# Two attentions in float32: key blocks that a DMA lays out, products on row halves and column strips of the array

## The reference

```
x = x + tanh(g_xattn[0]) * _L0_xattn_ref(_layernorm(x), ctx_512, ctx_512)   # 8 key heads of 8 numbers, 4 query heads each
x = x + tanh(g_ffn[0])   * _L0_ffn_ref(_layernorm(x), ...)                  # 64 experts, the best 8, and a shared one
x = x + tanh(g_xattn[1]) * _L1_xattn_ref(_layernorm(x), ctx_512, ctx_512, Wc, bc)  # 4 key heads of 16 numbers, 4 query heads each
x = x + tanh(g_ffn[1])   * _L1_ffn_ref(_layernorm(x), w_fc, w_proj)
# an attention: scores = einsum("bkgsd,bktd->bkgst", qh, kh) * scale; attn = softmax(scores); out = einsum("bkgst,bktd->bkgsd", attn, vh)
```

## Time and profile before

| | us |
|---|---|
| three runs | 1705.94, 1711.78, 1712.32 |
| their median | 1711.78 |
| span of the profiled execution | 1714.7 |

### The profile page before, as it was taken

One profiled execution on the slowest core, in us unless ns is written; L12 is line 12 of the kernel. 1 busy time (PEld: TensorE's weight loads), 2 busy tenths in 40 slices (PEclk: granted clock), 3 DMA queues, 4 the chain that ended last, 5 costly groups with the idle time before them and its releaser, 6 DMA issues.

```text
span 1714.7 us, 32329 instructions
## 1 busy us (share of the span) xinstructions
PE 1178.8 (69%) x9122; PEld 778.6 (45%) x9132; DVE 1084.7 (63%) x2699; ACT 783.1 (46%) x1599; POOL 883.5 (52%) x846
## 2 busy tenths in 40 slices
PE   4999998133333299999678777871676777846775
PEld 2566665112221266666555555650454444532243
DVE  5899996666666466666444454442765555747898
ACT  3566665122222166666445454441343333433574
POOL 2343343266666633333377777715888888516100
PEclk9999999555555599999777887785788888878878
DMA  9555554032323599999899999984344434100011
GB/s 209 161 151 154 148 154 135 15 115 104 111 106 110 154 281 308 310 301 304 206 242 237 252 246 248 247 199 101 53 54 55 55 55 55 28 1 1 13 37 49
DMA packets 283470, 247.09 MB, mean 144 GB/s; under 512 B 117584, under 2 KB 270032, under 8 KB 282960
## 3 DMA queue, kind: packets, MB, share of 16 engines
q1 hardware_dynamic: 234192, 169.99, 38.9%
q0 software_dynamic: 49152, 75.53, 20.8%
HBM read 111.93 MB, written 117.77 MB: 134 GB/s over the span
## 4 chain that ended last, share of the span: by engine, by line
DMA 24%; DVE 20%; PE 18%; POOL 16%; issue 13%; SPq 4%; ACT 3%; DVEq 1%; POOLq 0%; ACTq 0%
DMA xs<-V 13%; POOL x L632 11%; DMA arena<-xs 8%; PE bank L1493 4%; DVE arena L1318 3%; DMA xs<-arena,V 2%; PE bank L1369 2%; POOL rs L575 2%; PE bank L1381 2%; DVE arena L971 2%; PE bank L1355 2%; PE bank L1569 2%; PE bank L1370 2%; SPq L518 2%; DVE arena L1316 2%
## 5 line engine op out<-in xcount | busy, mean ns | idle before, releaser
L632 POOL DMA_INDIRECT x<-ys,idx x256 | 404.1, 1578 | 129.2 <-issue 57.6
L650 POOL DMA_INDIRECT xs<-V x192 | 187.1, 974 | 207.7 <-DMA xs<-V 188.5
L1493 PE MATMUL bank<-arena,region 128*128 128x128 f16 x2496 | 253.2, 245 | 1.6 <-ACT arena L834 0.9
L834 ACT COPY arena<-bank 128x640 f16<-128x640 f16 x192 | 132.3, 689 | 190.2 <-PE bank L1569 188.2
L1569 PE MATMUL bank<-arena 128*128 128x128 f16 x1440 | 145.2, 240 | 105.3 <-DMA arena<-xs 101.5
L1381 PE MATMUL bank<-arena 128*72 128x256 f32 (+1 forms) x768 | 212.0, 417 | 0.1
L1493 PEld LDWEIGHTS bank<-arena,region 128*128 (+1 forms) x2496 | 187.0, 111 | 19.2 <-issue 6.2
L1569 PEld LDWEIGHTS bank<-arena 128*128 128x128 f16 x1440 | 97.0, 107 | 113.3 <-DMA arena<-xs 85.4
L573 POOL TENSOR_TENSOR ve<-mv,epsilon 128x1 f32<-128x1 f32 x96 | 39.5, 412 | 202.0 <-DVE mv L912 180.0
L1381 PEld LDWEIGHTS bank<-arena 128*72 128x72 f32 (+1 forms) x768 | 117.2, 158 | 46.4 <-issue 13.5
L982 DVE TENSOR_REDUCE arena<-bank 128x8 f32<-128x512 f32 x192 | 124.1, 675 | 15.5 <-PE bank L1355 14.3
(11 more groups left out here) (204 smaller groups left out, 2557.6 us busy)
## 6 DMA issues: line engine op xcount, KB each, us to landing
ys<-arena SPq DMA_DIRECT2D x96, 512.0 KB
arena<-xs SPq DMA_DIRECT2D x288, 160.0 KB
xs<-idx SPq DMA_DIRECT2D x52, 256.0 KB, 2.4
arena<-in_wpairs SPq DMA_DIRECT2D x32, 256.0 KB, 2.6
arena<-in_wpairs SPq DMA_DIRECT2D x128, 64.0 KB, 2.5
x<-ys,idx POOLq DMA_INDIRECT x256, 6.3
out<-arena SPq DMA_DIRECT2D x16, 256.0 KB, 2.2
xs<-idx SPq DMA_DIRECT2D x52, 64.0 KB, 2.1
```

Source lines behind the costliest of these rows:

```text
L632: pool.indirect_dma_start(tile_x(t), None, ys[t // HT], bass.IndirectOffsetOnAxis(ap=idx[:, t, k:k + 1], axis=0), compute_op=ALU.add).then ...
L650: pool.indirect_dma_start(xs[t // HT], bass.IndirectOffsetOnAxis(ap=at_row[:, t, n % 8:n % 8 + 1], axis=0), ROW[t % NROW], None).then_inc( ...
L834: act.copy(XTP[g % 2][q], tpm[n % 2]).then_inc(R_["xt"], 1)
L1493: mm = pe.matmul(o, lhs(a, w, k), rhs(a, w, k), start=(n == 0), stop=(n == 3 * KT - 1))
```

## The change

- Queries, maxima and keys stay float32. The high and low parts go, and with them `KH`, `KL`, the mask table, L971, L1028, the casts of the keys and one of the two normalisations (`query`).
- Key blocks: four buffers `KD`, zeroed once. SP writes the diagonal blocks of a tile by DMA out of HBM, one DMA per key head (8 in layer 0, 4 in layer 1), each of 8 or 16 partitions by two runs of 64 numbers. The rows that take off the maximum come by 8 DMAs of their own per layer (`own_rows`). For layer 1, POOL zeroes the buffers after layer 0, and SP fills them in the middle of the experts (`g == NG`).
- The array is used in parts: half of the key heads on rows 0 to 63, the other half on rows 64 to 127, in two banks. Scores have 64 rows by 128 columns, maxima 32 rows by 64 columns, values 128 rows by strips of 32 (layer 0) or 64 columns (layer 1).
- Order: PE begins a step with the turning of tile `t + 2` and takes half of its maxima in step `t`. ACT casts the experts' weights at the end of a step, no longer between the exponentials. POOL fills `VD` in layer 0.

The core of the diff:

```diff
-    KH = sb("KH", [P, B, S], F16)
-    KL = sb("KL", [P, B, S], F16)
+    KD = [sb(f"KD{n}", [P, 2, 4 * S]) for n in range(NKD)]
...
-    XG = [carve([G, C + W0]) for _ in range(2)]
-    KM = carve([2 * 8 * S], F16)
-    Q1 = [carve([G, P], F16) for _ in range(2)]
-    Q2 = [carve([G, P], F16) for _ in range(2)]
-    KD1 = [carve([2, 8 * S], F16) for _ in range(2)]
-    KD2 = [carve([2, 8 * S], F16) for _ in range(2)]
-    VD = [carve([2, 4 * W0]) for _ in range(2)]
+    XG = [carve([G, P]) for _ in range(NKD)]
+    Q = [carve([G, P]) for _ in range(NKD)]
+    VD = [carve([2, P]) for _ in range(2)]
...
+            def own_rows(layer):
+                nk = LAYERS[layer][0]
+                a = CW + RCW + TCW + layer * 4 * S
+                for q in range(NKD):
+                    for r in range(2):
+                        at = slice(r * OWN + C // 2, r * OWN + C // 2 + nk // 2)
+                        sp.dma_start(KD[q][at, :, 0:nk // 2 * S],
+                                     consts[at, a:a + nk // 2 * S].unsqueeze(1).to_broadcast([nk // 2, 2, nk // 2 * S])).then_inc(d_own, 16)
+
+            def keys(t, layer):
+                nk, d = LAYERS[layer]
+                if t >= NKD:
+                    sp.wait_ge(A[layer]["sc_ready"], (t - NKD + 1) * nk // 2)
+                for k in range(nk):
+                    r, i = k // (nk // 2), k % (nk // 2)
+                    sp.dma_start(KD[t % NKD][r * OWN + i * d:r * OWN + (i + 1) * d, :, i * S:(i + 1) * S],
+                                 ctxT[k * d:(k + 1) * d, 2 * t * S:2 * (t + 1) * S].rearrange("c (b s) -> c b s", b=2)).then_inc(d_kd[t % NKD], 16)
...
+            sp.wait_ge(kd_zero, NKD)
+            own_rows(0)
+            for t in range(2):
+                keys(t, 0)
...
                 pair(n, stage[n], d_stage[n])
-            keys(1)
+            for t in range(2, NKD):
+                keys(t, 0)
             sp.dma_start(x[:, 4:12, :], xv[:, 4:12, :]).then_inc(d_x[1], 16)
             values(1)
             sp.dma_start(x[:, 12:NT, :], xv[:, 12:NT, :]).then_inc(d_x[2], 16)
...
+                if n + 2 < NT:
+                    keys(n + 2, 0)
                 sp.wait_ge(wlo_done, 2 * (n - 1))
                 if n > 2:
                     sp.wait_ge(d_w, 80 * (n - 2))
...
+                if g == NG:
+                    sp.wait_ge(kd_zero, 2 * NKD)
+                    own_rows(1)
+                    for t in range(NKD):
+                        keys(t, 1)
                 if NG <= g < NGG and (g - NG) % 6 == 0:
...
+            for t in range(NKD, NT):
+                keys(t, 1)
...
+                        if past(t, 0):
+                            pool.wait_ge(a["pv_ready"], t + 1)
+                            stand_alone(pool, side_v)
+                        pool.tensor_tensor(VD[j].rearrange("p b (n h w) -> p (b n) h w", h=2, w=P // nk)[:, :, :, 0:d],
+                                           V[:, bass.ds((t + 2) * 2, 2), :].rearrange("p b (n h d) -> p (b n) h d", h=2, d=d),
+                                           ones[:, 0:2].unsqueeze(1).unsqueeze(3).to_broadcast([P, 2 * npair, 2, d]), ALU.mult).then_inc(a["vd_ready"], 1)
...
+            for q in range(NKD):
+                pool.memset(KD[q][:, :, :].rearrange("p b t -> p (b t)"), 0.0).then_inc(kd_zero, 1)
...
+                def step(t, q):
+                    j = q % 2
+                    if inside(t + 2):
+                        act.wait_ge(a["t1_ready"], t + 3)
+                        act.copy(Q[(q + 2) % NKD], bank[0].rearrange("p (g s) -> p g s", g=G)).then_inc(a["q_ready"], 1)
                     if inside(t):
-                        for u in range(nsc):
+                        for u in range(2 * nsc):
                             exps(t, j, u)
...
-                    if inside(t):
-                        for u in range(nsc, 2 * nsc):
-                            exps(t, j, u)
...
+                    if layer == 0 and inside(t):
+
+                        if known(t) and t < 2:
+                            act.wait_ge(d_stage[t], 80)
+                        else:
+                            act.wait_ge(d_w, 80 * (t - 1))
+                        act.copy(gu_view(t, 0), stage[j][0].rearrange("p m e i -> p e m i")).then_inc(whi_done, 1)
+                        act.copy(RW[:, bass.ds(2 * t, 2), KT * P:SW], stage[j][1]).then_inc(whi_done, 1)
...
+                def first_step(t, q):
+                    j = q % 2
                     if inside(t + 1):
-                        for u in range(nmx // 2):
-                            maxima(t + 1, 1 - j, u)
+                        maxima(t + 1, (q + 1) % NKD, 0)
+                        maxima(t + 1, (q + 1) % NKD, 1)
+                    if inside(t + 3):
+                        if known(t) and t == -3:
+                            dve.wait_ge(d_x[0], 16)
+                        if known(t) and t in (1, 3):
+                            dve.wait_ge(d_x[(t + 1) // 2], 16)
+                        dve.bn_stats(st[:, 1 - j, :], tile_x(t + 3)).then_inc(LNA["stats"], 1)
...
+                        inverse(t - 1)
+                    if inside(t + 3):
+                        dve.wait_ge(LNA["stats"], t + 4)
+                        stand_alone(dve, side_v)
+                        dve.bn_aggr(mv[:, 1 - j, :], st[:, 1 - j, :]).then_inc(LNA["mv"], 1)
+                    if inside(t - 1):
+                        weighted(t - 1, 1 - j)
                     if inside(t + 1):
-                        for u in range(nmx // 2, nmx):
-                            maxima(t + 1, 1 - j, u)
+                        maxima(t + 1, (q + 1) % NKD, 2)
+                        maxima(t + 1, (q + 1) % NKD, 3)
...
+                def maxima(t, q, gp):
+
+                    n = t * nmx + 2 * gp
+                    if past(t, 1) or gp >= 1:
+                        pe.wait_ge(a["mx_done"], n)
+                    last = [None, None]
+                    for g in range(2 * gpu):
                         for b in range(2):
-                            mm = pe.matmul(bank[2 + u % 2][b * S:(b + 1) * S, g * nk * S:(g + 1) * nk * S],
-                                           Q1[j][:, u * gpu + g, b * S:(b + 1) * S], KD1[j][:, b, 0:nk * S],
-                                           start=True, stop=True)
-                    mm.then_inc(a["mx_ready"], 1)
...
+                            for r in range(2):
+                                rows = slice(r * OWN, r * OWN + C // 2)
+                                last[r] = pe.matmul(bank[2 + r][b * S:(b + 1) * S, g * hk * S:(g + 1) * hk * S],
+                                                    Q[q][rows, gp * 2 * gpu + g, b * S:(b + 1) * S], KD[q][rows, b, 0:hk * S],
+                                                    start=True, stop=True)
+                    for mm in last:
+                        mm.then_inc(a["mx_ready"], 1)
...
+                def scores(t, q, b):
+
+                    if layer == 0 and (past(t, 1) or b):
+                        pe.wait_ge(a["ex_ready"], t * 4 + 2 * b)
+                    if layer == 1 and past(t, 1) and b == 0:
+                        pe.wait_ge(a["ex_ready"], t * 2)
+                    last = [None, None]
+                    for p in range(nsc):
+                        for r in range(2):
+                            rows = slice(r * OWN, (r + 1) * OWN)
+                            at = (p if layer == 0 else b) * 256
+                            last[r] = pe.matmul(bank[4 + r][:, at:at + 256], KD[q][rows, b, p * P:(p + 1) * P],
+                                                Q[q][rows, :, b * S:(b + 1) * S], start=True, stop=True)
+                    if layer == 0 or b:
+                        for mm in last:
+                            mm.then_inc(a["sc_ready"], 1)
...
+                    cg = P // npair
                     for p in range(npair):
-                        e = EX[(b * nsc + p // 2 + (0 if nsc == 2 else 2 * j)) % 4]
-                        mm = pe.matmul(bank[6][0:w, b * 256:(b + 1) * 256], VD[j][:, b, p * w:(p + 1) * w],
-                                       e[:, (p % 2) * 256:(p % 2 + 1) * 256], start=(p == 0), stop=(p == npair - 1))
+                        e = EX[b * nsc + p // 2 if layer == 0 else p + 2 * j]
+                        at = (p % 2 if layer == 0 else b) * 256
+                        mm = pe.matmul(bank[6][p * cg:(p + 1) * cg, b * 256:(b + 1) * 256], VD[j][:, b, p * cg:(p + 1) * cg],
+                                       e[:, at:at + 256], start=True, stop=True)
...
+                def step(t, q):
+                    j = q % 2
+                    if inside(t + 2):
+
+                        pe.wait_ge(LNA["out"], ln + t + 3)
+                        if past(t, -1):
+                            pe.wait_ge(a["q_ready"], t + 2)
+                        if layer == 1 and past(t, 4):
+                            pe.wait_ge(F["xf_ready"], t - 3)
+                        for g in range(G):
```

(19 more changed lines are left out.)

292 lines of the change are left out of this document (110 added, 182 removed).

## The result

The changed kernel takes 1736.5 us (median of 4 runs, 1723.0 to 1738.7) where the kernel before takes 1710.7 in the same series (4 runs, 1705.9 to 1712.3): 1.4% slower, ratio 1.0142, 95% interval 1.0104 to 1.018. The profiled execution spans 1736.6 us, 21.9 more than before. The forecast was 1734. The total fits. The largest term in it fails, and a loss that was in no term makes up for it.

A forecast was written before the change was run, and what follows sets the result against it. It took PE to bound layer 0 before the change and SP's issue queue after it, POOL most of layer 1. Layer 0 +16, experts +8 and layer 1 -2 gave +22 on 1711.8, so 1734 us, range 1706 to 1775.

The forecast's parts named there:

- SP as the bound of layer 0: Layer 0: 8 more issues per iteration, 0.50 us each, use up SP's 3.2 us of waiting, so its queue sets the step.
- An iteration 9.0 us: SP's queue in layer 0: 5.0 + 8 x 0.50 = 9.0 us per iteration (8.1 to 10.1).
- rival 1: SP issues a small transfer in 0.39 us or a little less, iteration 8.1, total 1706 to 1720; chance 0.18.
- Layer 0, +16: Layer 0 gets 16 us longer: some 25 iterations +21, start +2, end -7.
- PE waits for the keys' DMA: Layer 0: PE waits for the keys (`d_kd`) at the last maxima of each step; no size given.
- PE's own step: Layer 0: PE alone would take 7.8 us a step, 6.8 of products and form changes plus about 1 of waiting.
- rival 3: Row halves of the array don't overlap: a step of 11.2 us, +92 in layer 0, total 1810; chance 0.10.
- rival 4: Maxima overlap in pairs only: a step of 9.5 us, +40 with the rest, total 1750; chance 0.08.
- DVE 5.5, the clock over 0.9: Layer 0 signs: DVE busy near 5.5 us per step; a clock under 0.9 would show the forecast wrong.
- Experts +8 (0 to +14): At group 48 SP issues 24 more transfers, 12 us, delaying the fetches: +8 us, bounds 0 and 14.
- Layer 1: "0 start, tail -2": Layer 1: POOL's extra memsets cost 0 at the start; PE's six tail steps give -0.3 each, -2 us (0 to -7).
- Sum: Whole kernel: 16 + 8 - 2 = +22 us, 1734 us on the median of the runs.

The follow-up runs named there:

- experiment 5: Changed kernel with half of layer 0's key issues left out from step 4 on, 4 instead of 8 per iteration: 1714.4 us, one run.
- experiment 7: Changed kernel with each of layer 0's key issues split in two, 16 of half the size per iteration: 1828.0 us, one run.
- experiment 11: Changed kernel with layer 1's PE order put back, its first keys ahead of the experts, ACT issuing four of layer 0's eight keys: 1692.8 us.
- experiment 3: Changed kernel with layer 1's first 24 own-row and key issues moved from group 48 to ahead of the experts: 1728.1 us.
- experiment 4: Changed kernel with layer 1's PE order put back and its first 24 own-row and key issues ahead of the experts: 1706.9 us.
- experiment 8: Changed kernel with both products of a score pair on the same upper row half of the array: 2009.1 us, one run.

## Why the prediction was right in sum and wrong in its parts

- **SP as the bound of layer 0.** Right in kind: no wait is left in its queue, 17 issues stand back to back, and experiments 5, 7 and 11 show that it sets the step. This is the first step that failed, and it failed by its size: I took 0.50 us for a slot, from the nearest rows, and measured are 0.35 (0.36 with its gap), the price that stood in the earlier trace rows as that of a pair's first issue and that I took for the exception. "An iteration 9.0 us" is 7.95, 8.16 on average: rival 1's slot.
- **Layer 0, +16.** It got 5 us shorter. By the starts of SP's pairs the loop begins 6.4 us later (45.41 against 39.02; forecast +2, bounds 0 to +10), the next 27 iterations take 3.6 us less (223.9 against 227.5; forecast some +21), and the end is 7.6 shorter (22.2 against 29.8; forecast -7). The iterations gain since the first four before take 9.5 to 10.6 us, not the 8.15 at which I priced all. The two issues of the start that I put down to full rings take 7.33 + 7.10 us where they took 15.35 + 5.65, so they did shrink when the 2 MB went. Whether a full ring was the reason no row shows.
- **PE waits for the keys' DMA.** Hardly, 0.8 us in 20 steps. The pair behind the keys comes late to ACT, ACT late to the exponentials, PE waits for ACT, 16 us in 20 steps. The direction was in the text, the place of the wait was not.
- **PE's own step.** Forecast 7.8, 7.6 where SP is relieved. The wait of about 1 us for DVE was smaller, 0.45, and the products take 7.2 us in place of 6.8 (37.76 of 40 us busy in experiment 11). The changes of form cost more than the 0.13 I took: four scores go on for 1.06 us (150.88 to 151.94) where two pairs at 0.43 stream 0.86, so 0.20, by the same count 0.14 to 0.17 for values and maxima. Row halves work side by side, maxima in fours, as assumed: rivals 3 and 4 did not come.
- **DVE 5.5, the clock over 0.9.** DVE is busy 124.81 us of 238, 4.2 per 7.95 us step, lower than I counted: the reductions take 2.5 of it. The normalisation that went, which I had counted at nothing, took 23.1 us in 20 steps before (L918), 1.16 a step, and that is nearly all of the difference. The clock is 0.97.
- **Experts +8 (0 to +14).** The 24 issues take 11.3 us (838.84 to 850.15; forecast 12), and PE stands 8.3 us longer behind them. The repeated runs give 8.4 and 8.9. Right, though the one slot of 0.50 is in fact 0.36 for the own rows and 0.52 for the keys.
- **Layer 1: "0 start, tail -2".** This is the second step that failed, and by its mechanism. I priced PE's stream alone, product by product, and that price was right: with the old order a step falls from 6.67 to 6.42, -0.25 where I had -0.3. I did not walk through the new order in layer 1, where the value products stand straight behind the scores whose exponentials they need, and the first turning straight behind the one that fills its bank. In layer 0 I did count DVE's chain against PE's cover. In layer 1 this was left out, and it costs 20.8 us in the medians (21.2 between experiments 3 and 4).
- **Sum.** Forecast +16 + 8 - 2 = +22, which adds up. Measured by the runs: order +21, keys at group 48 +8 to +9, everything else -3 (1706.9 against 1710.1). An error of -21 in layer 0 and one of +23 in layer 1 cancelled. So the total came out by luck, and was no evidence for the theory.

What stays open: how the order's 21 us divide between the waits themselves and the clock. Single profiles give 11.4 us for the waits in a tail at full clock. The rest lies in the gathers and in how often the tail starts at the lower clock, and no run holds the clock fixed.

## What to carry to other kernels

Price a reordered pipeline stage twice, once as the stream of its products and once as a walk along each engine's queue, asking at every instruction who wrote its input and how long ago. Do it for each loop that runs the order, since the order that suits one layer's banks and exponentials need not suit the other's. A queue that issues back to back is an engine like any other: add its issues up, and if it is the longest, give some of them to an engine with room.

## What the runs showed of the hardware

- In experiment 8 the granted clock reads 1.00 through the whole of layer 0, and PE is busy 240 of 240 us, yet every product has the length of the lower level (a turning 1.12 us, not 0.66) from the first at 17 us to the end of the stage at 548 us. All kernels begin so: in the changed one the turning takes 1.12 us at 29.03 and 0.66 at 34.95 (rows in experiment 8), and the granted clock of 0 to 40 us reads 1.00. In experiment 8 the column reads 1.00 on through the router and up to 1060 us, though five products of the experts' L1586 take 0.69 us at 854 and 0.44 at 1041. So the column says nothing ahead of its first change, and lengths of one form have to be compared. Why a PE that never pauses stays at the lower level, when only one row half works in its scores, is not settled. It is one run, so it may be chance.
- Issues of DMAs to 8 partitions take 0.34 us at 2 KB and 0.35 at 4 KB, from ACT's queue 0.28 to 0.40, and those to 16 partitions (8 KB) 0.46 to 0.52. A fill from 128 partitions takes 0.54, of twice the length 0.72 to 0.85, and the key issues behind it then 0.5 to 0.57 in place of 0.35.
- Four float32 products of 64 rows and 256 columns take 2.08 us in pairs on the two row halves and 3.78 in series on one, both at 1.2 GHz. At 2.4 GHz two of them take 0.70 side by side and 1.13 in series.
